# Relational count matrices of a graph network: turned by transposing DMA transfers instead of identity products on TensorE

## The chip, the cores and the metric

The kernel runs on 1 core of one Trainium2 chip. The metric is device time in microseconds of one execution. Three runs of the kernel before took 917.75 us in the median (916.77 to 920.0). A measurement of this kernel can tell a difference of about 0.3% (2.75 us) from none.

## What is computed

Four graph layers act on node features `x` of 1250 nodes by 512, over 21250 directed edges, each of which has one of two types. The third layer is relational: per edge type it has its own 512x512 weight (a mix of 30 basis matrices), a sigmoid gate per source node, and its own sum over neighbours. Cut to what matters here:

```python
edge_index = jnp.stack([src, dst])
x = _layernorm(x + _L0_gnn_ref(x, edge_index, ...))               # degree-normalised sum, batch norm, gelu
x = _layernorm(x + _L1_gnn_ref(x, src, dst, ...))                 # mean over neighbours, two layers
x = _layernorm(x + _L2_gnn_ref(x, edge_index, edge_type_2, ...))  # two rgcn_gate_layer
x = _layernorm(x + _L3_gnn_ref(x, edge_index, ...))               # sum over neighbours

def rgcn_gate_layer(x, row, col, edge_type, basis, att, gate_w, root, bias):
    w = jnp.einsum('rb,bio->rio', att, basis)
    x_j = x[col]
    msgs = [sigmoid(x_j @ gate_w[r, :, 0])[:, None] * x_j @ w[r] for r in range(2)]
    msg = jnp.where((edge_type == 0)[:, None], msgs[0], msgs[1])
    return segment_sum(msg, row, num_segments=N) + x @ root + bias
```

## The kernel before

All sums over neighbours are products with dense count matrices that the kernel builds first. Nodes are padded to 1280, ten tiles of 128. A **window** is 32 destination nodes, so there are 40 windows, four to a tile (`PER`).

**Counting.** For each window VectorE writes one-hot rows of the edges' keys (L1140, L1145, L1151) and TensorE multiplies them (L572, 8 products of 128x320 and 2 more for each further chunk; nearly all windows have 10 or 12 in all) into one of two sets of PSUM banks. ScalarE copies the sums out (`window_out`, L766) into `B`, a buffer for two tiles (j), laid out by source tile, then relation, then column: "p j s r c". TensorE may start window w when window w-2 is copied out (`s_wev`); VectorE may start window w when TensorE is done with window w-2 (`s_win`).

**What becomes of a tile of B.** VectorE adds both relations into `AT` (L1178, `sum_counts`), used by the non-relational layers. For the relational matrix `A` each 128x128 block has to be turned. TensorE does that: `turn_counts` (L597) multiplies four blocks by the identity into one PSUM bank, and ScalarE copies the bank into `A` (`turned_out`, L772). A tile takes five such **turns**, of 20 blocks in all. In the four windows that follow a tile they are done 1, 2, 1, 1 (`COUNT_STEPS`). The last tile's five turns stand inside the first dense products. `A` is first read by unit 3, far behind.

**Beside it.** Between windows TensorE also mixes the first relational layer's basis matrices (L620, 120 products of 128x512 in f32, two instructions each, here called mixes). SP loads a 256 KB matrix for each into 8 slots. Per window there are 2 or 3 mixes (`SHARES`), in eight groups of 15. A group's sum lies in the one bank `T[:, 1]`, and ScalarE copies it out (`mixed_out`, L779); TensorE may begin the next group, and after the last group the first dense product, only when this copy is done (`s_mxe`). Groups end in windows 5, 11, 17, 23, 28, 33 and 39. ScalarE further splits the input (`split_x`, L807 and L809, every second window from 19) and after window 35 the first weight (L863, L866).

**ScalarE's order** is the program's: per window `window_out`, turns out, `mixed_out`, `split_x`. It also issues transfers, among them the transposing ones that already exist (`turn_to`, L828: `S16` tile to a slot of `hT`, 128x1024 f16, 70 of them). Two are issued after window 38, two after window 39, and two at the start of unit 0. While a transfer is issued, what follows on ScalarE waits. The row label ACTq stands for this issuing.

**Unit 0** follows: ten dense tiles (L666), with a product that spreads the degrees (L708), then the aggregation (L721), out-degrees on ScalarE (L1010), batch norm, gelu. Units 1 to 6 follow.

Of the kernel before, what the change touches and what calls it, by code (L numbers as in the profile page):

```python
# [31 lines left out]
COUNT_STEPS = ((0,), (1, 2), (3,), (4,))  # L32
# [16 lines left out]
def resnorm_gnn_kernel(nc, x, src_t, dst_t, typ_t, dst_r, W0, b0, gamma, beta,  # L49
# [11 lines left out]
    with ctx:  # L61
# [101 lines left out]
        B = zview(2 * 2 * NT * REL * P).rearrange("p (j s r c) -> p j s r c", j=2, s=NT, r=REL)  # L163
# [50 lines left out]
        s_at = sem("s_at")  # L214
        s_ate = sem("s_ate")
# [9 lines left out]
        s_eye, s_mixT = sem("s_eye"), sem("s_mixT")  # L225
# [40 lines left out]
        b_idf, b_one, b_dg, b_row, b_rev = (sem("b_" + n) for n in ("idf", "one", "dg", "row", "rev"))  # L266
# [17 lines left out]
        def count_bank(t, g):  # L284

            return (T[:, 0, :], Dp[:, 0, 2, :])[(5 * t + g) % 2]

        LAST_BANKS = [Dp[:, 0, 1, :], Dp[:, 1, 1, :], Dp[:, 0, 2, :]]
# [143 lines left out]
        Z_SCALED = 38  # L432
# [134 lines left out]
        def _(pe):  # L567
# [24 lines left out]
            def turn_counts(t, g, bank):  # L592

                pe.wait_ge(s_wev, PER * (t + 1))
                for r in range(REL):
                    for i in range(2):
                        last = nc.tensor.matmul(bank[:, (2 * r + i) * P:(2 * r + i + 1) * P], B[:, t % 2, 2 * g + i, r, :],  # L597
                                                ident[:, :], start=True, stop=True)
                last.then_inc(s_at, 1)

# [38 lines left out]
            pe.wait_ge(s_mxe, GROUPS)  # L639

            for u, unit in enumerate(UNITS):
                nm, nz = len(unit["mats"]), unit["nz"]

                def dense(t, j):
# [28 lines left out]
                    if u == 0 and t == 0:  # L673
                        degrees(NT - 1)
                        for g in range(3):
                            turn_counts(NT - 1, g, LAST_BANKS[g])
                    if u == 0 and t == 2:
                        for g in range(3, 5):
                            pe.wait_ge(s_ate, 5 * (NT - 1) + g - 2)
                            turn_counts(NT - 1, g, LAST_BANKS[g - 3])  # L680
                    if u == 0 and t == 5:
                        pe.wait_ge(s_ate, 5 * NT)
# [880 lines left out]
```

## Time and profile before

| | us |
|---|---|
| median of 3 runs (lowest, highest) | 917.75 (916.77, 920.0) |
| the profiled execution | 917.2 |
| its span, first to last instruction | 915.4 |
| TensorE busy | 882.8 (96%) |
| VectorE busy | 656.2 (72%) |
| ScalarE busy | 280.8 (31%) |

The span is 1.8 us shorter than the execution's own time. The mean granted clock of TensorE is 0.985 of full speed. The counting stage lasts from 21 us to 184 us, unit 0's dense tiles from 184.6 to 214.

In the rows below, PE is TensorE's products, DVE VectorE, ACT ScalarE, ACTq and SPq the issuing of transfers on ScalarE and SyncE. A row of a timeline begins with start and duration in us; "x10" counts instructions that are merged in it, and the bracket at its end holds the idle time before it and what ended it. Ends of products are modelled: the next product starts before the row's end, so starts are compared with starts.

### The profile page before, as it was taken

How to read it: one execution, taken by the hardware profiler on the slowest of the kernel's cores; microseconds unless marked ns; L12 is line 12 of the kernel's file. 1: busy time of each engine (PE TensorE's matmuls, PEld its weight loads, DVE VectorE, ACT ScalarE, POOL GpSimd, SP SyncE). 2: the span in 40 equal slices, each digit the busy share in tenths (PEclk: the TensorE clock that was granted, in tenths of full speed). 3: DMA queues.
4: the chain of work that ended last, by engine and by line, in shares of the span. 5: the costliest groups of instructions: out<-in, count | busy, mean ns of one | idle time of the engine just before them, and what ended most of it. 6: DMA issues, size and time to landing. Idle time of an engine off the chain costs nothing.

```text
span 915.4 us, 12673 instructions
## 1 busy us (share of the span) xinstructions
PE 882.8 (96%) x4258; PEld 428.2 (47%) x4258; DVE 656.2 (72%) x1286; ACT 280.8 (31%) x431; POOL 87.9 (10%) x66
## 2 busy tenths in 40 slices
PE   7999999999959999899997999999999999999997
PEld 3555555554545444344443444444444444444443
DVE  6898978658987797998999988975324255552247
ACT  0333444637752116222312111114311221132221
POOL 1000111301220003021210000003200020020000
PEclk9999999999979999999998999999999999999999
DMA  8955665596435885788464655530131014322228
GB/s 275 352 168 165 183 188 191 149 238 198 155 95 157 200 236 150 208 207 204 128 150 108 155 141 161 139 91 1 35 81 23 12 47 139 82 62 41 47 60 237
DMA packets 134888, 129.50 MB, mean 141 GB/s; under 512 B 80687, under 2 KB 81156, under 8 KB 134826
## 3 DMA queue, kind: packets, MB, share of 16 engines
q10 hardware_dynamic: 96192, 60.25, 26.1%
q1 hardware_dynamic: 38634, 68.45, 24.9%
q8 instruction: 36, 0.59, 0.3%
q14 instruction: 26, 0.21, 0.1%
HBM read 97.80 MB, written 12.52 MB: 121 GB/s over the span
## 4 chain that ended last, share of the span: by engine, by line
PE 68%; DVE 15%; DMA 8%; ACT 4%; issue 2%; POOL 1%; DVEq 1%; ACTq 0%; SPq 0%
PE Dp L696 25%; PE Dp L666 24%; PE T L620 11%; PE Dp L572 6%; DVE acc L1262 4%; DMA stage<-in_basis 3%; DMA wst<-mixd 2%; DMA xr<-xres 2%; DVE Zraw L1373 1%; ACT W L1010 1%; DVE stt L1354 1%; ACT wst L863 1%; DVE w L1391 1%; PE T L666 1%; POOL Zraw L530 1%
## 5 line engine op out<-in xcount | busy, mean ns | idle before, releaser
L666 PE MATMUL Dp<-W,hT 128*128 128x512 f16 x792 | 175.7, 381 | 3.6 <-DMA hT<-S 3.6
L696 PE MATMUL Dp<-Zraw,A 128*128 128x512 f16 x800 | 173.0, 379 | 0.0
L1262 DVE SCALAR_TENSOR_TENSOR acc<-stage,att,acc 128x512 f32<-128x512 f32 x232 | 163.5, 770 | 4.3 <-DMA stage<-in_basis 4.3
L696 PE MATMUL Dp<-Zraw,AT 128*128 128x512 f16 x600 | 130.0, 379 | 0.0
L666 PEld LDWEIGHTS Dp<-W,hT 128*128 128x128 f16 x792 | 77.8, 98 | 96.6 <-DMA hT<-S 3.8
L696 PEld LDWEIGHTS Dp<-Zraw,A 128*128 128x128 f16 x800 | 78.2, 98 | 94.4
L696 PEld LDWEIGHTS Dp<-Zraw,AT 128*128 128x128 f16 x600 | 58.7, 98 | 70.8
L1140 DVE TENSOR_SCALAR Zraw<-hT,w 128x640 f16<-128x640 f16 (+1 forms) x209 | 85.9, 456 | 0.3
L1391 DVE SCALAR_TENSOR_TENSOR w<-Dp,aggc,S 128x512 f32<-128x512 f32 x40 | 29.9, 747 | 59.9 <-PE Dp L696 54.0
L962 ACT ACTIVATE Zraw<-Dp,zsc 128x512 f16<-128x512 f32 x46 | 29.4, 684 | 125.8 <-PE Dp L666 121.7
L620 PE MATMUL T<-stage,W 128*128 128x512 f32 x120 | 60.5, 627 | 5.5 <-DMA stage<-in_basis 5.5
L572 PE MATMUL Dp<-Zraw 128*128 128x320 f16 (+1 forms) x418 | 63.7, 299 | 0.4 <-DVE Zraw L1140 0.3
L1331 DVE SCALAR_TENSOR_TENSOR Zraw<-Dp,zsc,Zraw 128x512 f16<-128x512 f32 x26 | 19.5, 749 | 58.6 <-ACT Zraw L962 58.6
L1001 ACT ACTIVATE w<-w,s_in 128x512 f32<-128x512 f32 x30 | 21.6, 720 | 121.0 <-DVE w L1391 116.0
L530 POOL TENSOR_TENSOR W<-wst,W 128x1024 f16<-128x1024 f32 x18 | 42.8, 2395 | 158.6 <-ACT W L866 158.6
L572 PEld LDWEIGHTS Dp<-Zraw 128*128 128x128 f16 (+1 forms) x418 | 40.6, 98 | 36.9 <-issue 23.2
L620 PE MATMUL T<-Zraw,W 128*128 128x512 f32 x120 | 57.4, 601 | 0.0
L666 PE MATMUL Dp<-W,stage 128*128 128x512 f16 x240 | 52.8, 379 | 1.2 <-DVE Zraw L1331 1.2
L766 ACT ACTIVATE Zraw<-Dp 128x640 f16<-128x640 f32 x40 | 28.1, 703 | 78.4 <-PE Dp L572 76.3
L721 PE MATMUL Dp<-AT,Zraw 128*128 128x512 f16 (+1 forms) x240 | 43.4, 344 | 0.0
L1151 DVE TENSOR_TENSOR Zraw<-hT,Zraw 128x512 f16<-128x512 f16 x40 | 28.5, 712 | 20.8 <-PE Dp L572 15.0
L962 ACT ACTIVATE Zraw<-Dp 128x512 f16<-128x512 f32 x26 | 15.5, 596 | 74.6 <-PE Dp L666 72.0
(176 smaller groups left out, 950.4 us busy)
## 6 DMA issues: line engine op xcount, KB each, us to landing
stage<-in_basis SPq DMA_DIRECT2D x180, 256.0 KB, 2.9
Zraw<-in_basis SPq DMA_DIRECT2D x60, 256.0 KB, 3.1
xres<-w ACTq DMA_DIRECT2D x30, 256.0 KB, 2.3
xr<-xres ACTq DMA_DIRECT2D x30, 256.0 KB, 3.1
wst<-in_Wn ACTq DMA_DIRECT2D x4, 1024.0 KB, 5.6
wst<-in_Ws ACTq DMA_DIRECT2D x4, 1024.0 KB, 6.0
wst<-mixd ACTq DMA_DIRECT2D x4, 1024.0 KB, 6.0
wst<-in_root ACTq DMA_DIRECT2D x3, 1024.0 KB, 6.7
```

The source lines that it names most:

```text
L530: pool.tensor_tensor(weights_of(u, m)[:, 1, 2 * h:2 * h + 2, :], source, weights_of(u, m)[:, 0, 2 * h:2 * h + 2, :], ALU.subtract).then_in ...
L572: last = nc.tensor.matmul(Dp[:, j, b, 0:HALF], oh_lo[:, ds(slot * P, P)], oh_key[:, ds(slot * KEYS + b * HALF, HALF)], start=start, stop=stop)
L620: nc.tensor.matmul(T[:, 1, :], mixT[:, b * P:(b + 1) * P], mix_in[n % MIX_SLOTS], start=(b == 0), stop=(b == PAIRS - 1)).then_inc(s_mx, 1)
L666: last = nc.tensor.matmul(dense_bank(u, t, m), turned[:, hp, k * P:(k + 1) * P], weights_of(u, m)[:, wp, k, :], start=(n == 0), stop=(n == ...
L696: last = nc.tensor.matmul(sum_bank(t), a[:, k, ds(t * P, P)], Z[:, r, h, k, :], start=(n == 0), stop=(n == count - 1))
L721: last = nc.tensor.matmul(Df[:, j, c:c + w], Z[:, 0, h, k, b * P:(b + 1) * P], AT[:, k, c:c + w], start=(k == 0 and h == 0), stop=(k == NT ...
L766: nc.scalar.activation(B[:, t % 2, :, :, a:a + WIN].rearrange("p s r (b d) -> p b (s r) d", b=2), Dp[:, w % 2, 0:2, 0:HALF].rearrange("p b ...
L962: nc.scalar.activation(Z[:, r, 0, ds(t, 1), :], dense_rows(u, t, r), ACT.Copy, scale=scale).then_inc(s_zhi[u], 1)
L1140: return v.tensor_scalar(oh_key[:, ds(slot * KEYS, KEYS)], iota_n, wkey[:, w:w + 1], key_f[:, ds(c, 1)], ALU.add, ALU.is_equal)
L1151: v.tensor_tensor(oh_lo[:, slot * P:(slot + n) * P].rearrange("p (c k) -> p c k", c=n), iota_n[:, 0:P].rearrange("p (c k) -> p c k", c=1). ...
L1262: last = v.scalar_tensor_tensor(part, stage[:, q, :], a, part, ALU.mult, ALU.add)
L1391: v.scalar_tensor_tensor(w1[:, j:j + 1, :], sum_bank(t).rearrange("p (a d) -> p a d", a=1), c, rest, ALU.mult, ALU.add).then_inc(s_pre[u], 1)
```

## The change

`turn_counts`, `turned_out`, `count_bank`, `COUNT_STEPS` and the semaphores `s_at` and `s_ate` go. In their place ScalarE issues, once the four windows of a tile are copied out, two transposing transfers (`move_counts`), one for each relation, from `B` to `A`: 128x1280 f16 each, 20 in all. `B` is laid out by relation first ("p j r s c"), so that a relation's counts lie in a row; keys are numbered accordingly. Waits on `s_moved` take the place of those on `s_ate`: before ScalarE overwrites a half of `B`, before VectorE's aggregation work of unit 0 (whose data overlay `B`), and before TensorE's first relational aggregation in unit 3. `s_eye` and `b_idf` are folded into the common chain of VectorE.

```diff
-COUNT_STEPS = ((0,), (1, 2), (3,), (4,))
+MOVED = (0, 1)
-        B = zview(2 * 2 * NT * REL * P).rearrange("p (j s r c) -> p j s r c", j=2, s=NT, r=REL)
+        B = zview(2 * 2 * NT * REL * P).rearrange("p (j r s c) -> p j r s c", j=2, s=NT, r=REL)
@@ tensor
-                    for g in COUNT_STEPS[w % PER]:
-                        wait(pe, s_ate, 5 * t + g - 1)
-                        turn_counts(t, g, count_bank(t, g))
                     if w % PER == 2:
                         degrees(t)
                 mix(mix_share(w))
             assert mixed[0] == PAIRS * GROUPS
-            pe.wait_ge(s_ate, 5 * (NT - 1))
             pe.wait_ge(s_mxe, GROUPS)
...
+                    if u == 3 and t == 0:
+                        for i in range(2):
+                            pe.wait_ge(s_moved[i], 16 * len(MOVED) * NT // 2)
@@ scalar, window_out
                 if t > 1 and w % PER == 0:
-                    act.wait_ge(s_ate, 5 * (t - 1))
+                    act.wait_ge(s_moved[t % 2], 16 * len(MOVED) * (t // 2))
@@ scalar
-            def turned_out(t, g, bank):
-                act.wait_ge(s_at, t * 5 + (g + 1))
-                nc.scalar.activation(A[:, :, t, 2 * g * P:2 * (g + 1) * P], bank.rearrange("p (r c) -> p r c", r=REL),
-                                     ACT.Copy).then_inc(s_ate, 1)
+            def move_counts(t):
+
+                act.wait_ge(s_wev, PER * (t + 1))
+                for r in MOVED:
+                    act.dma_start_transpose(A[:, r, t, :].rearrange("p (s n) -> p s n", s=NT),
+                                            B[:, t % 2, r, :, :].rearrange("p s c -> p (s c)")).then_inc(s_moved[t % 2], 16)
@@ scalar, tile_out
                     window_out(w)
-                    if t:
-                        for g in COUNT_STEPS[i]:
-                            turned_out(t - 1, g, count_bank(t - 1, g))
                     if w == NWIN - 1:
                         turn_to(4, 0)
+                    if i == PER - 1:
+                        move_counts(t)
                     for g in range(groups_done(w - 1) if w else 1, groups_done(w)):
                         mixed_out(g)
@@ vector, keys
-            link(v.tensor_copy(key_f, typ_i))
+            link(v.tensor_scalar(key_f, typ_i, float(NT), None, ALU.mult))
...
-            link(v.scalar_tensor_tensor(key_f, src_f, float(REL) / P, key_f, ALU.mult, ALU.add))
+            link(v.scalar_tensor_tensor(key_f, src_f, 1.0 / P, key_f, ALU.mult, ALU.add))
```

ScalarE at the end of the counting stage, windows 36 to 39 and the start of unit 0, in the kernel before:

```order
109 L766 ACTIVATE Zraw<-Dp 128x2x20x16
110 L772 ACTIVATE A<-T 128x2x256
111 L766 ACTIVATE Zraw<-Dp 128x2x20x16
112 L772 ACTIVATE A<-Dp 128x2x256
113 L772 ACTIVATE A<-T 128x2x256
...
118 L828 DMA_TRANSPOSE w<-S 128x8x128 x2
119 L766 ACTIVATE Zraw<-Dp 128x2x20x16
120 L772 ACTIVATE A<-T 128x2x256
121 L828 DMA_TRANSPOSE xr<-S 128x8x128 x2
122 L779 ACTIVATE gw<-T 128x512
123 L782 DMA mixd<-gw 64x512 x2
```

And in the changed kernel, whose L742 is `window_out`, L750 `move_counts`, L757 `mixed_out`, L784 and L786 `split_x`, L805 `turn_to` (`Zraw` holds `B`):

```order
56 L742 ACTIVATE Zraw<-Dp 128x2x20x16 x2
57 L750 DMA_TRANSPOSE A<-Zraw 128x10x128 x2
58 L784 ACTIVATE w<-xr,s_in 128x512
59 L786 ACTIVATE S<-w 128x512
60 L840 ACTIVATE wst<-wst,sW 128x1024 x2
61 L843 ACTIVATE W<-wst 128x1024 x2
62 L742 ACTIVATE Zraw<-Dp 128x2x20x16 x2
...
67 L742 ACTIVATE Zraw<-Dp 128x2x20x16
68 L805 DMA_TRANSPOSE xr<-S 128x8x128 x2
69 L750 DMA_TRANSPOSE A<-Zraw 128x10x128 x2
70 L757 ACTIVATE gw<-T 128x512
```

The copies of turned banks are gone, and behind windows 35 and 39 two longer transposing transfers stand ahead of the splits and ahead of the copy of the last mixed group. Earlier, the same pair stands behind every fourth window; behind windows 11 and 23 it is ahead of `mixed_out` too.

## Rows read from the trace of the kernel before

**Rows 1.** The page: the chain that ended last, by engine.
```profile
PE 68%; DVE 15%; DMA 8%; ACT 4%; issue 2%; POOL 1%; DVEq 1%; ACTq 0%; SPq 0%
```

**Rows 2.** Busy time by stretch: length, PE, PEld, DVE, ACT, POOL, PEclk, DMA share, GB/s.
```profile
60.00:80.00 20.00, 19.63 (x119) 10.91 (x118) 18.62 (x41) 7.05 (x12) 1.24 (x2) 1.00 0.57 166
120.00:160.00 40.00, 40.00 (x220) 22.58 (x219) 31.63 (x78) 17.81 (x31) 5.84 (x4) 1.00 0.58 185
```

**Rows 3.** Timeline of PE: products of windows 1, 2, 7, 8 and 37.
```profile
24.11 1.52 PE L572 MATMUL Dp<-Zraw 128*128 128x320 f16 x10
...
28.04 1.52 PE L572 MATMUL Dp<-Zraw 128*128 128x320 f16 x10
...
46.75 1.52 PE L572 MATMUL Dp<-Zraw 128*128 128x320 f16 x10
...
50.96 1.52 PE L572 MATMUL Dp<-Zraw 128*128 128x320 f16 x10
...
171.21 1.52 PE L572 MATMUL Dp<-Zraw 128*128 128x320 f16 x10
```

**Rows 4.** Timeline of DVE, first keys of windows 8, 9, 14; PE's window 14.
```profile
44.85 0.69 DVE L1151 TENSOR_TENSOR Zraw<-hT,Zraw 128x512 f16<-128x512 f16 x1 [0.74 <-PE Dp L572]
48.49 0.69 DVE L1151 TENSOR_TENSOR Zraw<-hT,Zraw 128x512 f16<-128x512 f16 x1 [1.00 <-PE Dp L572]
...
73.54 0.69 DVE L1151 TENSOR_TENSOR Zraw<-hT,Zraw 128x512 f16<-128x512 f16 x1 [0.62 <-issue]
...
75.09 1.95 PE L572 MATMUL Dp<-Zraw 128*128 128x320 f16 x10 [0.27 <-DVE Zraw L1140]
```

**Rows 5.** Timeline, windows 23 and 24: PE's products, ACT's copy of a mixed group.
```profile
111.08 1.52 PE L572 MATMUL Dp<-Zraw 128*128 128x320 f16 x10
...
115.49 0.60 ACT L779 ACTIVATE gw<-T 128x512 f32<-128x512 f32 x1 [1.66 <-PE T L620]
```

**Rows 6.** Timeline of PE, window 35, and of ACT behind it until window 36 is out.
```profile
163.37 1.52 PE L572 MATMUL Dp<-Zraw 128*128 128x320 f16 x10
...
166.01 0.72 ACT L807 ACTIVATE w<-xr,s_in 128x512 f32<-128x512 f32 x1
...
167.30 2.17 ACT L863 ACTIVATE wst<-wst,sW 128x1024 f32<-128x1024 f32 x2
...
171.27 0.68 ACT L766 ACTIVATE Zraw<-Dp 128x640 f16<-128x640 f32 x1
```

**Rows 7.** Timeline: PE in windows 38 and 39, ACT, and PE's first dense product.
```profile
175.65 1.52 PE L572 MATMUL Dp<-Zraw 128*128 128x320 f16 x10
...
179.28 1.52 PE L572 MATMUL Dp<-Zraw 128*128 128x320 f16 x10
...
184.57 2.75 PE L666 MATMUL Dp<-W,w 128*128 128x512 f16 x12 [0.91 <-issue]
...
182.47 1.30 ACTq L828 DMA_TRANSPOSE xr<-S  x1
183.87 0.60 ACT L779 ACTIVATE gw<-T 128x512 f32<-128x512 f32 x1 [1.84 <-PE T L620]
```

**Rows 8.** Timeline of ACT: issuing of transposing transfers, 128x1024 f16 each.
```profile
185.73 1.51 ACTq L828 DMA_TRANSPOSE hT<-S  x1
...
187.28 3.34 ACTq L828 DMA_TRANSPOSE hT<-S  x1
...
363.38 1.25 ACTq L828 DMA_TRANSPOSE Zraw<-S  x1
```

**Rows 9.** Busy time by stretch, columns as in rows 2: one microsecond of such transfers.
```profile
179.00:180.00 1.00, 1.00 (x8) 0.53 (x6) 0.00 (x0) 0.00 (x0) 1.00 (x2) 1.00 1.09 207
```

**Rows 10.** Chain that ended last, in order of time: a window's products, the last tile's turns.
```profile
167.75 1.63 PE Dp L572 x12
...
187.55 0.69 PE Dp L597 x12
...
193.42 0.45 PE Dp L597 x8
```

More of the change, by code:

```diff
@@ L213, in resnorm_gnn_kernel @@
         s_wev = sem("s_wev")
-        s_at = sem("s_at")
-        s_ate = sem("s_ate")
+        s_moved = [sem(f"s_moved{j}") for j in range(2)]
         s_xin, s_xmax, s_s0 = sem("s_xin"), sem("s_xmax"), sem("s_s0")
@@ L224, in resnorm_gnn_kernel @@
         e_att = sem("e_att")
-        s_eye, s_mixT = sem("s_eye"), sem("s_mixT")
+        s_mixT = sem("s_mixT")
         mx_full = [sem(f"mx_full{i}") for i in range(MIX_SLOTS)]
@@ L265, in resnorm_gnn_kernel @@
         s_xst = {u: [sem(f"s_xst{u}_{j}") for j in range(2)] for u in LN}
-        b_idf, b_one, b_dg, b_row, b_rev = (sem("b_" + n) for n in ("idf", "one", "dg", "row", "rev"))
+        b_one, b_dg, b_row, b_rev = (sem("b_" + n) for n in ("one", "dg", "row", "rev"))
         b_ev, b_st, b_mv, b_sd, b_co, b_g = (sem("b_" + n) for n in ("ev", "st", "mv", "sd", "co", "g"))
@@ L431, in resnorm_gnn_kernel @@
         XS_FROM = 19
-        Z_SCALED = 38
+        Z_SCALED = 39
         def halves_split(u):
@@ L590, in window @@
                 pair_product(FIXED * (w % 2) + 1, j, stop=True).then_inc(s_win, 1)
[L592 to L599, printed above, removed]
             def degrees(t):
@@ L674, in dense @@
                         degrees(NT - 1)
[L675 to L680, printed above, removed]
                     if u == 0 and t == 5:
-                        pe.wait_ge(s_ate, 5 * NT)
                         spread()
@@ L763, in window_out @@
                 if t > 1 and w % PER == 0:
-                    act.wait_ge(s_ate, 5 * (t - 1))
+                    act.wait_ge(s_moved[t % 2], 16 * len(MOVED) * (t // 2))
                     act.wait_ge(s_sum, 2 * (t - 1))
-                nc.scalar.activation(B[:, t % 2, :, :, a:a + WIN].rearrange("p s r (b d) -> p b (s r) d", b=2),
+                nc.scalar.activation(B[:, t % 2, :, :, a:a + WIN].rearrange("p r s (b d) -> p b (r s) d", b=2),
                                      Dp[:, w % 2, 0:2, 0:HALF].rearrange("p b (d k) -> p b k d", k=REL * NT),
                                      ACT.Copy).then_inc(s_wev, 1)
-            def turned_out(t, g, bank):
-                act.wait_ge(s_at, t * 5 + (g + 1))
-                nc.scalar.activation(A[:, :, t, 2 * g * P:2 * (g + 1) * P], bank.rearrange("p (r c) -> p r c", r=REL),
-                                     ACT.Copy).then_inc(s_ate, 1)
+            def move_counts(t):
[3 more added lines that the diff above has]
+                                            B[:, t % 2, r, :, :].rearrange("p s c -> p (s c)")).then_inc(s_moved[t % 2], 16)
             def mixed_out(g):
@@ L980, in first_z @@
                     z_out(t, j)
-                    if u == 0 and t in (0, 2):
-                        for g in range(3) if t == 0 else range(3, 5):
-                            turned_out(NT - 1, g, LAST_BANKS[g % 3])
                     if u == 0 and t == 6:
@@ L1087, in _ @@
             dve.wait_ge(s_const, 8)
-            v.tensor_tensor(eye, ident[:, 0:P // 2], ident[:, P // 2:P], ALU.add).then_inc(s_eye, 1)
-            dve.wait_ge(s_eye, 1)
+            link(v.tensor_tensor(eye, ident[:, 0:P // 2], ident[:, P // 2:P], ALU.add))
             def mix_table(a0, a1):
@@ L1177, in sum_counts @@
                 dve.wait_ge(s_wev, PER * (t + 1))
-                v.tensor_tensor(AT[:, :, t * P:(t + 1) * P], B[:, t % 2, :, 0, :], B[:, t % 2, :, 1, :], ALU.add).then_inc(s_sum, 1)
+                v.tensor_tensor(AT[:, :, t * P:(t + 1) * P], B[:, t % 2, 0, :, :], B[:, t % 2, 1, :, :], ALU.add).then_inc(s_sum, 1)
                 dve.wait_ge(s_sum, 2 * t + 1)
@@ L1314, in _ @@
                 dve.wait_ge(s_mxst[j], 16 * REL * GROUPS // 2)
-            v.tensor_copy(identf, ident[:, :]).then_inc(b_idf, 1)
-            dve.wait_ge(b_idf, 1)
+            link(v.tensor_copy(identf, ident[:, :]))
             for t in range(NT):
@@ L1482, in _ @@
                     dve.wait_ge(s_bn, 48)
+                    for i in range(2):
+                        dve.wait_ge(s_moved[i], 16 * len(MOVED) * NT // 2)
                     weight_work("agg", 0, 0)
```

4 lines of the change are left out of this document (removed).

## The prediction

> **What bounds the kernel now.** I read the chain of waits first: two thirds of it lie on TensorE [rows 1]. The change touches TensorE only in the counting stage (21 to 184 us) and in unit 0's first dense tiles, so the busy times by stretch come next. TensorE is busy all the time from 120 to 160, while VectorE has 31.6 of 40 us and ScalarE 17.8; from 60 to 80 VectorE is at 18.6 of 20 too [rows 2]. So the reader is to see a stage bound by TensorE, with a stretch in it where VectorE has almost no room. The timelines of both engines then say what a turn costs and where VectorE waits, and ScalarE's timeline says what it holds when others wait for it.
>
> **What a turn costs TensorE.** Windows 1, 7 and 37 each have 10 window products and 3 mixes until the next window starts, and 0, 1 and 2 turns. From start to start they take 28.04 - 24.11 = 3.93, 50.96 - 46.75 = 4.21 and 175.65 - 171.21 = 4.44 us [rows 3, 7]. A turn is 0.28 us where it stands alone, two are 0.51. Twelve window products run 1.63 us [rows 10], so ten run 1.36 and a mix (3.93 - 1.36) / 3 = 0.86. A tile's five in windows with 1, 2, 1, 1 are 3 x 0.28 + 0.51 = 1.35; I take 1.3, as the third of these windows has the degree product too, and keeps a part of the change-over between kinds of product. Nine tiles hold 11.7 us of turns in the counting stage. The copies that go from ScalarE (45 there, 5 later) are not on the path.
>
> **How much of that VectorE lets through.** VectorE waited for TensorE 0.74 and 1.00 us before windows 8 and 9, then works without such a wait until window 14's keys, which TensorE waits for itself, by 0.27 us [rows 4]. A faster TensorE brings VectorE to window 14 earlier by at most those 1.74 us, and TensorE has saved about 1.3 by window 8: I take **1.0 us** at window 14 (bounds 0 and 1.74). From there to window 39 are 25 windows, 6.25 tiles: 6.25 x 1.3 = **8.1 us**. In windows 15 to 20 VectorE is still near its limit; of the two, one catches the other again, and I take **1.0 us** off (bounds 0 and 2.5, the saving of two tiles). TensorE would reach the end of window 39 earlier by 1.0 + 8.1 - 1.0 = 8.1 us, if nobody else held it.
>
> **What the moves cost ScalarE.** The kernel has 70 transposing transfers of 128x1024. Their issue holds ScalarE 1.25 us where the queue is empty, 1.30 in a row of four, and 1.51 and 3.34 when the basis loads of the next stage press on it [rows 7, 8]. No row shows one of 128x1280. If issue goes by size it is 1.56, if it doesn't it is 1.25; beside the basis loads of the counting stage, which take 0.57 of the transfer engines [rows 2], I take **1.7 us**. The lower end is 1.25, the upper 3.34. As for the transfers themselves, 1.09 of the 16 engines' time gave 207 GB/s [rows 9], so 327,680 bytes take some 1.6 us and two per tile 3.3 in each 15 us: the share goes from 0.57 to about 0.8. The mixes' loads have eight slots, some 12 us of work ahead. I cost that at nothing; if that cover goes, TensorE waits for basis matrices.
>
> A pair is issued when its window's copy is done, some 1.0 us after the window's last product, so it holds ScalarE until 1.0 + 3.4 = 4.4 us behind that. Queued behind it are the copy of a mixed group, the splits and the next window's copy. Four places matter.
> - **Window 11.** The group's copy comes late, but what TensorE loses is lost before window 14, where it waits for VectorE anyway: nothing.
> - **Window 23.** It ends at 111.08 + 1.36 = 112.44 and the copy of the group came at 115.49, just behind the mixes [rows 5]. Now it is done at 4.4 + 0.6 + 0.1 = 5.1 us behind the window. TensorE wants the bank after 3 mixes of 0.86 and window 24's twelve products (1.63): 4.2. Cost **0.9 us**.
> - **Window 35.** It ends at 164.73. A split (1.4) and the first weight's scaling (167.30 to 171.27, 4.0) came ahead of window 36's copy [rows 6]. With the pair it begins at 4.4 + 1.4 + 4.1 = 9.9 and is seen at 10.8 us. Window 38 needs it, and TensorE, without turns, is there at 2.57 + 1.63 + 1.71 + 1.36 + 2.57 = 9.8. Cost **1.0 us**.
> - **Window 39.** It ends at 180.64. Four transposing transfers were issued until 183.77, then the last group was copied and the first dense product began at 184.57, 3.93 us behind the window [rows 7]. The pair now goes between: the first at 1.7 as elsewhere, the second under the basis loads of the next stage, which start with the last mix. The 3.34 us of rows 8 is the second in that state; with less queued I take 3.1. So 3.13 + 0.1 + 4.8 + 0.8 for the copy and its hand-overs is 8.8 us, and the cost is 8.8 - 3.9 = **4.9 us** (bounds 2.6 with two issues of 1.25, and 6.8 with two of 3.34).
>
> **The dense tiles.** TensorE goes through the last tile's turns in 0.69 + 0.45 = **1.1 us** [rows 10], which are rows of the chain that ended last, so this is gained. Dense tile 4 needs tile 0 of the first aggregation's input from ScalarE and VectorE; ScalarE has the fifth and sixth turned tile to issue ahead of that, as before. Unit 0's later steps start from the end of the dense tiles and shift with them. The waits on `s_moved` ask for data that landed long ago. The new order of `B` changes no instruction's size.
>
> **The sum.** -8.1 + 0.9 + 1.0 + 4.9 - 1.1 = -2.4 us. Against the profiled execution that is 917.2 - 2.4 = 914.8; this execution lies 0.55 below the median, so on the scale of the medians it is **915.3 us**. All that hangs on one number: with every issue at x us the three stalls are 2(x - 1.25), 2(x - 1.2) and 2x + 0.1, and the sum is 6x - 14.0.
>
> **Two rules of the Trainium skill.** Rows 3 give 0.28 us for four blocks on TensorE, and rows 9 some 1.6 us of all transfer engines for ten. "VectorE: DVE Perf Modes" (Rules for kernel authors) advises TensorE for turning 128x128 where PSUM will do as the place of the result, and the transfer otherwise. It speaks against this change, and rows 3 and 9 agree with its direction; by it the moves are the dearer path, which is the second rival. "Advanced Engine Details and Errata" (X-Bar Transpose (TRN2)) says transposing transfers run as fast as plain ones, at 350 to 400 GB/s. The 207 GB/s of rows 9 don't agree; by its figure a move would take an estimated 0.8 to 0.9 us and hardly queue, which is the first rival.
>
> **Rivals.**
> - *No back-pressure, the last pair costs what others do.* At 1.56 us each, 6 x 1.56 - 14.0 = -4.6; at 1.25, -6.5. That is 911.2 to 913.1. For it: four in a row went at 1.25 to 1.34 without one being held. Against: 3.34 in rows 8, in that very place.
> - *Transfers hold ScalarE everywhere; slower.* From x = 2.33 on the sum is positive. The ring may be short, and each pair is issued beside 256 KB loads. At 3.0 it is +4.0, and group copies at window 28 come late too, about +5.5: 921.8 to 923.3. TensorE's idle time would stand ahead of mixes, put down to ScalarE's copy. Against: the rows with light traffic show 1.25.
> - *VectorE becomes the bound.* If it binds until window 24, where before it waited little, 2.5 us instead of 1.0 are lost: -0.9, 916.9; with a call on the loads, 918.
>
> **How the numbers follow.** Forecast (913.2 to 917.5) 0.45, no back-pressure 0.25, back-pressure everywhere 0.17, VectorE or loads 0.13. About 0.3% (2.75 us) is what a measurement can tell. Faster by more than that, below 915.0: all of the second case and four tenths of the first, 0.25 + 0.17 = 0.42. Slower, above 920.5: most of the third case and a little of the last, 0.20. The same: 0.38. The range reaches from the first rival's best, 910.8, to 922.0, which takes in most of the second and leaves out its worst.
>
> **What would show it.** In the changed profile: windows 7 and 37 some 0.28 and 0.5 us shorter; window 14 earlier by about 1 us and the end of window 39 by about 6, at 174.4; issues of `move_counts` near 1.7 us, the last near 3; TensorE idle ahead of the first dense product for some 5 us, put down to ScalarE or to issue; the transfer share between 120 and 160 near 0.8. I am wrong if an issue takes over 2.3 us in the middle of the stage, if TensorE waits for basis matrices, or if the end of window 39 moves by less than 4 us.

## The result, and the profile after

| | us |
|---|---|
| after: median of 4 runs (lowest, highest) | 933.42 (929.44, 935.47) |
| before: median of 4 runs (lowest, highest) | 917.87 (916.77, 920.0) |
| ratio (95% interval) | 1.0168 (1.0142 to 1.0193) |
| the profiled execution after, its span | 935.15, 933.3 |

The changed kernel is slower by some 15.5 us. The forecast was 915.3 with a range up to 922.0, so the prediction was wrong, in sign too. The changed kernel also spreads more: its four runs lie 6.0 us apart, those of the kernel before 3.2.

**Where the time went.** The chain that ended last, by engine (it answers to [rows 1]):

```profile
PE 61%; DVE 16%; DMA 6%; ACTq 6%; ACT 6%; issue 2%; POOL 1%; SPq 0%; DVEq 0%
```

ScalarE's issuing (ACTq) went from 0% to 6% of the span, TensorE from 68% to 61%. What TensorE waited for between 5 and 300 us (engine and line, what it waited for, total us, times, longest us):

```profile
PE Dp L647 <- ACT gw L757: 10.5, 1, 10.5
PE T L605 <- DMA stage<-in_basis: 6.4, 2, 5.4
PE Dp L566 <- ACT Zraw L742: 5.0, 3, 3.1
PE T L605 <- ACT gw L757: 4.4, 2, 2.4
```

Of the 6.4 us on basis matrices 5.4 lie at the start and stand in the kernel before too (5.5). The rest is new: 10.5 us ahead of the first dense product (L647), 5.0 us ahead of window products (L566) and 4.4 us ahead of mixes (L605), all on a copy of ScalarE, and 1.1 us on a basis matrix. ScalarE's timeline says why those copies are late:

```profile
33.60 11.36 ACTq L750 DMA_TRANSPOSE A<-Zraw  x2
45.01 1.30 ACT L742 ACTIVATE Zraw<-Dp 128x640 f16<-128x640 f32 x2 [11.44 <-issue]
...
52.83 9.16 ACTq L750 DMA_TRANSPOSE A<-Zraw  x2
...
104.02 3.41 ACTq L750 DMA_TRANSPOSE A<-Zraw  x2
...
118.38 4.40 ACTq L750 DMA_TRANSPOSE A<-Zraw  x2
123.21 0.60 ACT L757 ACTIVATE gw<-T 128x512 f32<-128x512 f32 x1 [4.86 <-issue]
...
187.60 2.85 ACTq L805 DMA_TRANSPOSE xr<-S  x2
190.49 7.73 ACTq L750 DMA_TRANSPOSE A<-Zraw  x2
198.33 0.60 ACT L757 ACTIVATE gw<-T 128x512 f32<-128x512 f32 x1 [10.10 <-issue]
```

The ten pairs of moves held ScalarE 11.36, 9.16, 6.40, 3.39, 3.41, 4.40, 3.45, 3.41, 3.76 and 7.73 us. In the middle of the stage a move costs mostly 1.7 us, as forecast (2.2 in the sixth pair); in the first three pairs and the last it costs about two to three times that. The shortest single issue took 1.35 us. At the end of the stage, on TensorE (it answers to [rows 7]):

```profile
184.38 1.52 PE L566 MATMUL Dp<-Zraw 128*128 128x320 f16 x10
...
198.98 4.42 PE L647 MATMUL Dp<-W,w 128*128 128x512 f16 x12 [10.51 <-ACT gw L757]
...
203.49 2.75 PE L647 MATMUL Dp<-W,w 128*128 128x512 f16 x12
```

Window 39's products end at 184.38 + 1.36 = 185.74 (before 180.64, forecast 174.4), and the first dense product starts 13.24 us behind that (before 3.93, forecast 8.8). The first twelve dense products then take 4.42 us and the next 2.75: after the long idle time TensorE started at the lower level of its clock (the mean from 190 to 200 is 0.61, see below; from 199 to 202 it is 0.50). The clock fell at two more places, inside the counting stage. The rows are a window behind a wait of 3.09 us, two mix instructions behind a wait of 2.05 us (elsewhere 1.52 and 1.02 us), and the stretch from 124 to 125 with a granted clock of 0.50:

```profile
45.77 2.85 PE L566 MATMUL Dp<-Zraw 128*128 128x320 f16 x10 [3.09 <-ACT Zraw L742]
...
123.86 2.07 PE L605 MATMUL T<-stage,W 128*128 128x512 f32 x2 [2.05 <-ACT gw L757]
```

```profile
124.00:125.00 1.00, 1.00 (x2) 0.48 (x3) 0.54 (x1) 0.00 (x0) 0.00 (x0) 0.50 1.27 288
```

Up to the next window's start they cost some 1.4 us (4.77 instead of the 3.41 that the same products take from 165.10) and 1.8 us (4.36 instead of 2.58 for three mixes).

Busy time by stretch, columns as in [rows 2], of the kernel before:

```profile
20.00:30.00 10.00, 10.00 (x45) 5.41 (x44) 6.56 (x24) 2.41 (x4) 0.00 (x0) 1.00 1.03 375
30.00:40.00 10.00, 10.00 (x49) 5.47 (x49) 7.95 (x21) 2.20 (x4) 0.00 (x0) 1.00 1.06 385
40.00:50.00 10.00, 10.00 (x62) 5.78 (x60) 8.27 (x24) 4.67 (x8) 0.00 (x0) 1.00 0.69 215
60.00:70.00 10.00, 10.00 (x60) 5.73 (x59) 9.96 (x22) 4.05 (x7) 0.35 (x1) 1.00 0.56 162
```

and after:

```profile
40.00:50.00 10.00, 6.91 (x30) 3.37 (x30) 5.47 (x16) 2.49 (x4) 0.00 (x0) 0.83 1.15 199
...
60.00:70.00 10.00, 7.84 (x41) 3.52 (x40) 9.51 (x22) 2.22 (x4) 0.00 (x0) 1.00 1.20 126
...
120.00:160.00 40.00, 37.95 (x171) 20.21 (x170) 30.98 (x75) 12.70 (x20) 5.23 (x4) 0.96 0.85 224
...
190.00:200.00 10.00, 1.02 (x3) 0.43 (x4) 0.00 (x0) 0.60 (x1) 0.00 (x0) 0.61 1.11 201
```

From 40 to 80 us the transfer engines are busy throughout (1.13 to 1.20, where 0.56 to 0.69 stood before), and between 60 and 70 they move fewer bytes, 126 GB/s instead of 162. Between 120 and 160 the share is 0.85; I had said about 0.8.

### The profile page after: what moved, and what is told of

It reads as the page before. It is cut to its first block, busy times and chain, and to the rows that moved or that the text cites. A ratio compares the mean times of both kernels' runs of the same rounds, so it can differ in the third digit from the quotient of the medians.

```text
span 933.3 us, 12200 instructions
## 1 busy us (share of the span) xinstructions
PE 877.0 (94%) x4058; PEld 416.9 (45%) x4058; DVE 656.3 (70%) x1286; ACT 256.2 (27%) x381; POOL 86.7 (9%) x66
## 4 chain that ended last, share of the span: by engine, by line
PE 61%; DVE 16%; DMA 6%; ACTq 6%; ACT 6%; issue 2%; POOL 1%; SPq 0%; DVEq 0%
PE Dp L673 24%; PE Dp L647 22%; PE T L605 8%; PE Dp L566 5%; DVE acc L1235 5%; ACTq L750 5%; DMA stage<-in_basis 2%; DVE stt L1326 1%; DVE Zraw L1345 1%; ACT wst L840 1%; ACTq L805 1%; ACT W L984 1%; DMA wst<-mixd 1%; DVE w L1363 1%; DMA xr<-xres 1%
## 5 line engine op out<-in xcount | busy, mean ns | idle before, releaser
L647 PE MATMUL Dp<-W,hT 128*128 128x512 f16 x792 | 176.9, 383 | 3.8 <-DMA hT<-S 3.5
L647 PEld LDWEIGHTS Dp<-W,hT 128*128 128x128 f16 x792 | 77.8, 98 | 97.8 <-issue 3.8
L566 PE MATMUL Dp<-Zraw 128*128 128x320 f16 (+1 forms) x418 | 65.7, 303 | 6.1 <-ACT Zraw L742 5.0
L605 PE MATMUL T<-stage,W 128*128 128x512 f32 x120 | 61.4, 633 | 8.5 <-DMA stage<-in_basis 6.4
L566 PEld LDWEIGHTS Dp<-Zraw 128*128 128x128 f16 (+1 forms) x418 | 40.7, 99 | 44.6 <-issue 23.3
L605 PE MATMUL T<-Zraw,W 128*128 128x512 f32 x120 | 57.6, 603 | 2.4 <-ACT gw L757 2.4
L647 PE MATMUL Dp<-W,stage 128*128 128x512 f16 x240 | 52.8, 379 | 1.2 <-DVE Zraw L1303 1.2
L742 ACT ACTIVATE Zraw<-Dp 128x640 f16<-128x640 f32 x40 | 27.7, 700 | 86.1 <-PE Dp L566 57.6
L647 PE MATMUL Dp<-W,wst 128*128 128x512 f16 x144 | 34.2, 402 | 4.9 <-DVE S L1311 4.9
```

The costliest lines, as they stand in the source:

```text
L566: last = nc.tensor.matmul(Dp[:, j, b, 0:HALF], oh_lo[:, ds(slot * P, P)], oh_key[:, ds(slot * KEYS + b * HALF, HALF)], start=start, stop=stop)
L605: nc.tensor.matmul(T[:, 1, :], mixT[:, b * P:(b + 1) * P], mix_in[n % MIX_SLOTS], start=(b == 0), stop=(b == PAIRS - 1)).then_inc(s_mx, 1)
L647: last = nc.tensor.matmul(dense_bank(u, t, m), turned[:, hp, k * P:(k + 1) * P], weights_of(u, m)[:, wp, k, :], start=(n == 0), stop=(n == ...
```

## The experiments

Theory 1: what ScalarE's queue holds while a move is issued is the cost, above all where other loads press on the transfer engines, and behind window 39. 1a says that it is the turning that makes a move dear there, 1b that any transfer of that size would be. The rivals are the new layout, VectorE as the bound, and missing basis matrices. Times of before in the same sessions were 917.29 to 918.17 in the median. "Gap" is the time from the end of window 39's products to the first dense product. Where a kernel has added lines, its line numbers differ.

| kernel | time (median) | ratio (interval) | w14 out | w39 ends | gap |
|---|---|---|---|---|---|
| before | 917.87 | 1 | 77.08 | 180.64 | 3.93 |
| after | 933.42 | 1.0168 (1.0142 to 1.0193) | 84.98 | 185.74 | 13.24 |
| plain copies | 911.79 | 0.9931 (0.9914 to 0.9947) | 76.93 | 173.93 | 5.35 |
| no moves | 912.09 | 0.9935 (0.9911 to 0.9959) | 76.16 | 175.03 | 4.50 |
| few loads (one run) | 920.22 | | 76.81 | 175.29 | 11.23 |
| first two tiles turned | 920.6 | 1.003 (1.0018 to 1.0041) | 77.63 | 176.95 | 10.69 |
| last pair late | 923.2 | 1.0057 (1.0036 to 1.0079) | 82.19 | 182.91 | 5.31 |
| groups first | 921.98 | 1.0046 (1.0027 to 1.0065) | 81.87 | 182.20 | 4.23 |
| spread | 917.97 | 0.9996 (0.9979 to 1.0013) | 78.31 | 178.82 | 4.41 |
| hybrid | 915.51 | 0.9965 (0.9949 to 0.9982) | 76.83 | 177.44 | 5.17 |
| hybrid, GpSimd later | 913.38 | 0.9954 (0.9935 to 0.9972) | 77.73 | 178.92 | 5.85 |
| the same, copy first | 913.22 | 0.9955 (0.9939 to 0.997) | 76.39 | 174.33 | 3.48 |

(Window 14's copy starts and window 39's products end at the times given, in us of the profiled execution. That execution can lie off the median: for "GpSimd later" it took 921.38 us, the slowest of seven, so the three places in its row are not typical of it.)

**Only the layout.** The kernel before, with the diff's new order of `B` and of the keys:

```diff
-        B = zview(2 * 2 * NT * REL * P).rearrange("p (j s r c) -> p j s r c", j=2, s=NT, r=REL)
+        B = zview(2 * 2 * NT * REL * P).rearrange("p (j r s c) -> p j r s c", j=2, s=NT, r=REL)
```

> The kernel before with the second part of the change alone: B and the keys lie by relation first, and TensorE turns the blocks as before. Theory: the order of B costs nothing, since no copy, sum or product changes its size: copies of a window 0.70 us, sums 0.82 us, 917 to 919 us, the same. Rival: the window's copy or the sum into AT is dearer or cheaper by its new strides; 0.2 us on each of 40 copies or 10 sums would move the time by 1 us or more.

It took 918.21 us, ratio 0.9998 (0.9979 to 1.0018). The order of `B` costs nothing.

**Moves left out, first try.** `move_counts` and the waits on it go, and GpSimd fills `A` with zeros:

```diff
             pool.memset(ones, 1.0).then_inc(b_one, 1)
+            pool.memset(A[:, :, :, :].rearrange('p r t n -> p (r t n)'), 0.0).then_inc(b_one, 1)
...
-                    if i == PER - 1:
-                        move_counts(t)
```

> The changed kernel without its 20 moves: A is set to zero by GpSimd once instead (part left out: the relational counts). Theory 1 (the moves' issue holds ScalarE, and TensorE waits for the copies queued behind it): without them TensorE keeps what the turns cost: end of window 39 some 8 us before the kernel before's 180.6 (172 to 173), first dense product 3.9 us behind it, whole kernel 9.2 us faster than before: about 908.6. Rival (VectorE is the limit once the turns are gone): window 39 ends at 176 or later and the kernel is at 912 or above.

It took 931.92 us, ratio 1.0147 (1.0129 to 1.0165), for a cause that I had put in myself. GpSimd's timeline, and the waits of TensorE:

```profile
11.46 21.52 POOL L513 MEMSET A<- 128x25600 f16 x1
```

```profile
PE Dp L567 <- DVE Zraw L1108: 22.5, 4, 18.0
```

While GpSimd filled `A` for 21.5 us, one small operation of VectorE ahead of its first keys (L1090, 128x40) took 21.52 us instead of 0.18. The keys came late by that, and TensorE waited up to 18.0 us for them. As a test of the moves it says nothing; its gap, 199.56 - 195.08 = 4.5 us, is that of the next kernel.

**Moves left out, second try.** No filling; the relational sums read `AT` instead:

```diff
-                    rels = [(A[:, r], r) for r in range(REL)] if nz == 2 else [(AT, 0)]
+                    rels = [(AT, r) for r in range(REL)] if nz == 2 else [(AT, 0)]
...
-                    if i == PER - 1:
-                        move_counts(t)
```

> The changed kernel without any move; the relational sums read AT in place of A, which has the same shape (part left out: the relational counts). Step of the prediction under test: what the turns cost TensorE and how much of it VectorE lets through. By the prediction window 39 is out 8.1 us before the kernel before and the kernel takes 908.6. With what e2_plain_copies showed (window 39 out 6.7 us earlier, no gain at window 14), 908 to 910. Rival (the plain copies of e2 cost nothing, VectorE alone took the difference): within 1 us of e2_plain_copies, 911 to 912.

912.09 us, with no wait on ScalarE inside the counting stage. The prediction's 908.6 and the theory's 908 to 910 were missed; the rival's number came, within 1 us of the plain copies below. This is the change without its price. Window 14 came 77.08 - 76.16 = 0.92 us earlier, window 38 7.4 us earlier (169.78 instead of 177.20), and window 39 5.6 us. The last two microseconds went to a collision. VectorE's keys of window 39, and GpSimd beside them:

```profile
169.28 2.11 DVE L1112 TENSOR_SCALAR Zraw<-hT,w 128x128 f16 x1
171.31 3.00 DVE L1107 TENSOR_SCALAR Zraw<-hT,w 128x640 f16 x3
```

```profile
169.13 4.29 POOL L524 TENSOR_TENSOR W<-wst,W 128x1024 f16<-128x1024 f32 x2
```

The keys at L1112 take 0.24 and the three at L1107 1.15 us elsewhere. In the kernel before, GpSimd's subtractions (the low parts of the first weight) ran from 176.91, when VectorE's last keys had been written. They start straight behind GpSimd's own part of the last input split. Without two copies of turned banks between window 37's copy and that split they start 3.3 us behind window 37's copy instead of 4.1, and VectorE's keys of window 39 start 1.9 us behind it instead of 0.8, so the two meet. "SBUF — State Buffer" of the Trainium skill (SBUF: two separate sides) says that for VectorE operations of some kinds (those in a two-port mode, and some with two inputs in SBUF) and any GpSimd operation, whichever starts first holds the ports that they share for its whole instruction. 2.11 us beside GpSimd instructions of some 2.1 us each agrees with it; that the keys are of such a kind is not shown otherwise.

**Plain copies of the same bytes.** This leaves the number, the size and the place of the transfers, and takes the turning away:

```diff
-                    act.dma_start_transpose(A[:, r, t, :].rearrange("p (s n) -> p s n", s=NT),
-                                            B[:, t % 2, r, :, :].rearrange("p s c -> p (s c)")).then_inc(s_moved[t % 2], 16)
+                    act.dma_start(A[:, r, t, :],
+                                  B[:, t % 2, r, :, :].rearrange("p s c -> p (s c)")).then_inc(s_moved[t % 2], 16)
```

> The changed kernel with each move as a plain SBUF-to-SBUF copy of the same 327,680 bytes, at the same places on the same queue (part left out: the turning). Theory 1a (it is the transposing kind of transfer that is slow and holds its issuer when the basis loads press): issues of 0.3 to 1 us each, no waits of TensorE for ScalarE's copies, 908 to 911 us. Rival 1b (any transfer of this size that meets SP's loads is held): the first three pairs and the last one hold ScalarE 5 to 11 us as in the changed kernel, 925 to 933 us.

911.79 us, just outside the theory's 908 to 911: all but nothing is lost against the kernel without moves. One wait of TensorE for ScalarE is left, 2.61 us ahead of the first dense product. Its timelines of ScalarE and TensorE:

```profile
33.01 1.17 ACTq L750 DMA_DIRECT2D A<-Zraw  x2
```

```profile
179.28 2.76 PE L647 MATMUL Dp<-W,w 128*128 128x512 f16 x12 [2.61 <-ACT gw L757]
```

Where the turning pair held ScalarE for 11.36 us, two plain copies take 1.17, in the same traffic. The third part of the profiles' pages gives the engine time: the queue of these transfers has 26.1% of 915.4 us before, 28.5% of 911.0 with plain copies and 31.0% of 933.3 after. Twenty plain copies add 20.7 us, 1.0 each; twenty moves add 50.4, 2.5 each, where I had estimated 1.6 (part of this may be other transfers of that queue that take longer beside them). That is 1a; 1b falls. The two kinds differ in one more thing: a move adds 1312 packets to its queue, some 250 bytes each, and a plain copy 144, some 2.3 KB each. A plain copy in packets of that size was not run, so whether it is the turning or the small packets that are dear stays open.

**Few loads.** The moves as in the changed kernel, but only the first eight basis matrices are loaded:

```diff
-                for n in range(first, end):
+                for n in range(first, min(end, MIX_SLOTS)):
```

> The changed kernel with only the first 8 of the 120 basis matrices of the first relational layer loaded; the other mixes read the same slots again (part left out: their data). The moves then meet an idle queue, but for the x tiles at the start and the next stage's loads at the last pair. Theory 1 (basis loads of SP hold the moves): each pair holds ScalarE about 3.1 us or less, the first one too, TensorE waits for ScalarE by 2 us or less before window 39, which is out before 176. Rival 1d (a transposing transfer of this size holds its issuer by itself): first pairs of 6 us and more as in the changed kernel. The time isn't compared with 917, since loads are missing; window 39 and the pairs are.

One run took 920.22 us. The first pair and one in the middle, and one microsecond of such transfers alone:

```profile
32.98 3.13 ACTq L751 DMA_TRANSPOSE A<-Zraw  x2
...
96.88 2.95 ACTq L751 DMA_TRANSPOSE A<-Zraw  x2
```

```profile
99.00:100.00 1.00, 1.00 (x9) 0.77 (x8) 1.00 (x5) 0.12 (x1) 0.00 (x0) 1.00 1.08 200
```

Nine pairs take 2.91 to 3.81 us (11.36 has become 3.13), and only the last, beside the loads of the next stage, 6.96. So it is the moves beside loads that hold ScalarE for long. TensorE waited 1.8 us for ScalarE's copies before window 39, as the theory said. Alone, a pair occupies all engines for 0.96 + 1.08 + 1.15 + 0.31 = 3.5 us between 98 and 102, 1.75 us per move at 188 to 208 GB/s. Here the second issue of a pair takes 2.95 - 1.35 = 1.6 us, about as long as one move occupies the engines. That it waits for the first move to get through is my reading; no row shows the wait itself.

**The last pair late.** Only the last tile's pair goes behind dense tile 8's output:

```diff
-                    if i == PER - 1:
+                    if i == PER - 1 and t < NT - 1:
                         move_counts(t)
...
                     z_out(t, j)
+                    if u == 0 and t == 8:
+                        move_counts(NT - 1)
```

> The changed kernel with only the last tile's pair moved to another place: behind dense tile 8 of unit 0, in place of ahead of the last mixed group's copy. Prices the turnover. Theory 1: the first dense product starts some 4 to 5 us behind window 39's last product (13.2 in the changed kernel), the time falls by 8 to 9 us: 923 to 926. Rival (the transposing transfers of the next tiles are themselves held by the basis loads): it starts 8 us or more behind, 928 or above.

923.2 us, 933.4 - 923.2 = 10.2 us less, and the gap is 5.31. Not all of it is the last pair's place. In the profiled executions the gap is 7.9 us shorter and the dense tiles 1.3 us (the clock stays up), 9.3 together. But window 39 already ends 2.8 us earlier, though up to there the two programs are the same: the first pair takes 12.54 us, the second and third 4.57 and 3.55, where the changed kernel's took 9.16 and 6.40. How long early pairs are held differs from execution to execution by that much.

**The first two tiles turned.** Tiles 0 and 1 are turned on TensorE as before, the other pairs stay where the change puts them:

```diff
-                    if i == PER - 1:
+                    if i == PER - 1 and t >= TURNED:
                         move_counts(t)
```

> The changed kernel with tiles 0 and 1 turned by TensorE as before, all others in pairs at the places of the changed kernel. Prices the first two pairs, which held ScalarE 11.4 and 9.2 us. Theory 1: window 14 is out at 77 to 78 (84.98 in the changed kernel; VectorE's own time), so 6 to 8 us come back: 925 to 928. Rival (the third pair and the later ones take over what the first two cost): 930 or above.

920.6 us: the first two pairs cost 12.8 us, against 6 to 8 expected. Window 14 is back at 77.63, and the third pair shrank with them, from 6.40 to 4.11:

```profile
65.45 4.11 ACTq L780 DMA_TRANSPOSE A<-Zraw  x2
...
180.31 6.53 ACTq L780 DMA_TRANSPOSE A<-Zraw  x2
```

10.2 and 12.8 add up to 23.0, more than the 21.3 us between the changed kernel and the one without moves. By places of the profiled executions, window 39 ends 8.8 us earlier here, and 2.6 more come from a shorter gap, though the last pair stands where it was. So each price carries some 2 to 3 us that are not its own, and I read them as about half and half.

**Groups first.** The copy of a mixed group goes ahead of the pair:

```diff
-                    if i == PER - 1:
-                        move_counts(t)
                     for g in range(groups_done(w - 1) if w else 1, groups_done(w)):
                         mixed_out(g)
+                    if i == PER - 1:
+                        move_counts(t)
```

> The changed kernel with the copy of a finished mixed group ahead of the tile's moves on ScalarE; nothing else is changed. Theory 1: TensorE's waits for that copy go (4.4 us in the counting stage, 10.5 ahead of the first dense product), but the last pair, held some 8 us, now delays the turned tiles 4 and 5 and the first output of the dense tiles, so about 4 us come back as a wait inside the dense tiles: 920 to 924 us. Rival 2 (load on the transfer engines is the cost, wherever ScalarE stands): the time hardly moves, 930 or more.

921.98 us, inside the theory's range. The gap is back at 4.23, but the pair, which holds ScalarE for 4.88 us, now delays the outputs of the first dense tiles, and TensorE waits 2.5 us at dense tile 4. In the counting stage its waits for the group copies go, and 4.1 us of waits for window copies stay. The first pairs take 10.56 and 7.33 us, much as before. The fourth and fifth take 7.42 and 7.60 us, where the changed kernel's took 3.39 and 3.41, in the middle of the stage. The fourth pair is issued at 89.40 there and at 86.28 here. The first whole microsecond behind the issue, in the changed kernel and in this one:

```profile
90.00:91.00 1.00, 1.00 (x3) 0.29 (x2) 1.00 (x4) 0.00 (x0) 0.00 (x0) 1.00 0.35 39
```

```profile
87.00:88.00 1.00, 1.00 (x4) 0.36 (x3) 1.00 (x3) 0.00 (x0) 0.00 (x0) 1.00 0.98 332
```

There it met a gap between two bundles of basis loads, here it met a bundle. So the middle of the stage isn't cheap by itself; what a pair costs goes with the traffic at its moment of issue.

**Spread.** One move at a time, behind windows 4t + 4 and 4t + 6; the last tile's behind the outputs of dense tiles 7 and 8:

```diff
-                    if i == PER - 1:
-                        move_counts(t)
...
+                    if t and i in (0, 2):
+                        move_counts(t - 1, (i // 2,))
...
                     z_out(t, j)
+                    if u == 0 and t in (7, 8):
+                        move_counts(NT - 1, (t - 7,))
```

> The changed kernel with its moves issued one at a time: of each tile the first behind the first window of the next tile, the second behind its third, always behind the copy of a mixed group; the last tile's two behind dense tiles 7 and 8. Theory 1 (a second transfer issued behind a first that hasn't moved holds ScalarE): issues near 1.35 us, hardly any wait of TensorE for ScalarE, 909 to 913 us, so faster than before. Rival 2 (20 transfers of about 2.5 us of all engines' time starve the mixes of basis matrices): TensorE waits for those loads by 5 us or more and the time is 917 or above.

917.97 us, ratio 0.9996: the theory's 909 to 913 was missed. A single issue takes 1.35 to 1.5 us mostly, but not among the first:

```profile
43.80 5.27 ACTq L750 DMA_TRANSPOSE A<-Zraw  x1
```

A move then landed up to 15.6 us after its issue, so that window 8's copy waited for the buffer `B` until 59.52 (52.52 before), and window 39 lost more to the collision with GpSimd. The time is near the rival's, by another mechanism: TensorE waited only 1.6 us for basis matrices.

**Hybrid.** Spread, and tiles 0 and 1 turned on TensorE.

> Tiles 0 and 1 of B are turned by TensorE as in the kernel before (their moves met the saturated transfer engines, 20 to 60 us); tiles 2 to 9 are moved one transfer at a time as in e4_spread. Theory 1 (loss comes from moves issued into a busy queue, and ten turns ahead of window 14, where TensorE waits for VectorE anyway, cost nothing): issues of 1.35 to 1.5 us, window 39 out at 173 to 175 (180.84 in the kernel before, 179.02 in e4_spread), 910 to 913 us. Rival 2 (the load of transposing transfers on the engines costs TensorE's loads wherever they stand): 916 or above.

915.51 us, ratio 0.9965 (0.9949 to 0.9982): the first version that beats the kernel before by a measurable amount, though the interval doesn't exclude less than the 0.3% that I had named. It missed the theory's 910 to 913, and window 39's copy starts at 177.65, not 173 to 175. Issues take 1.34 to 2.46 us, 1.4 in the median. It has the collision with GpSimd:

```profile
170.19 3.44 DVE L1148 TENSOR_SCALAR Zraw<-hT,w 128x640 f16<-128x640 f16 x2
173.56 2.11 DVE L1153 TENSOR_SCALAR Zraw<-hT,w 128x128 f16 x1
```

```profile
171.25 4.37 POOL L532 TENSOR_TENSOR W<-wst,W 128x1024 f16<-128x1024 f32 x2
```

**GpSimd later.** The hybrid, and GpSimd's subtractions wait for the last keys:

```diff
+            pool.wait_ge(s_oh, FIXED * NWIN)
             low_weights(0, 0)
```

> e5_hybrid with one more wait: GpSimd starts the low half of the first weight only when VectorE has written its last keys. In e5 and e6 two 128x1024 subtractions of GpSimd (4.4 us) run while VectorE writes window 39's keys, and a key operation there takes 2.1 to 2.6 us in place of 0.25 to 0.4. Theory 3 (the two engines hold each other up, and window 39 is late by that): keys back at 0.25 to 0.4 us, window 39 out near 175 (177.65 in e5), 912 to 914 us. Rival (GpSimd's result, now later, is what the first dense product waits for): window 39 is out earlier but the first dense product still starts near 182.6, 915 to 916.

913.38 us, ratio 0.9954 (0.9935 to 0.9972). The keys at those two lines take 0.80 and 0.25 us again, so the collision is gone; the interval overlaps the hybrid's, so the 2.1 us between the medians are likely, not shown. Its profiled execution, the slow one of 921.38 us, doesn't show the earlier end of window 39 (its copy starts at 181.02). The next kernel, which is the same up to there, does: 175.45, as forecast.

**Copy first.** In window 39 the last group's copy also goes ahead of the turned input tiles:

```diff
-                    if w == NWIN - 1:
-                        turn_to(4, 0)
                     for g in range(groups_done(w - 1) if w else 1, groups_done(w)):
                         mixed_out(g)
+                    if w == NWIN - 1:
+                        turn_to(4, 0)
```

> e9b_pool_later with the copy of the last mixed group ahead of the two transposing transfers that are issued behind window 39. Theory 1 (what stands ahead of that copy on ScalarE is what the first dense product waits for, transfers of before included): the first dense product starts 3.9 to 4.2 us behind window 39's last product (5.9 in e9b), 911 to 913 us, against 917.4 of the kernel before. Rival (dense tiles 2 to 5 then wait for their turned input, issued later by 0.7 to 1 us): the start moves, the end of the dense tiles doesn't, and the time is that of e9b, 913 to 914.

913.22 us, ratio 0.9955. TensorE's timeline and waits:

```profile
177.81 2.75 PE L670 MATMUL Dp<-W,w 128*128 128x512 f16 x12 [0.73 <-ACT gw L788]
```

```profile
PE T L670 <- DMA xr<-S: 1.4, 1, 1.4
```

The gap is 3.48, the shortest of all, but dense tile 2 waits 1.4 us for its turned input, which stands behind the copy now. The gain of one wait went into another, as the rival said. This version and the one before it are some 4 to 5 us faster than the kernel before and 20 faster than the changed one. The kernel before with only this last order of copies was not run.

## Why the prediction was wrong

**What held.**
- *The turns' price.* Windows of 10 products and 3 mixes take 3.93 us, as said. The kernel without moves gained 6.5 us between windows 14 and 38 (7.4 - 0.92), where 7.1 net was forecast up to window 39.
- *Window 14 is pinned by VectorE.* 1.0 was forecast, 0.92 measured; without moves TensorE waits 2.63 us for VectorE there (0.27 before).
- *Windows 23 and 35.* 0.9 and 1.0 us were forecast. TensorE's waits there were 2.05 us (at 123.86, on the copy of the group) and 0.72 us (at 180.61, on window 36's copy): 2.8 instead of 1.9.
- *The dense tiles.* From the first dense product to the aggregation it took 29.49 before and 28.39 with plain copies, 1.1 less, as forecast.
- *The layout.* Nothing, as said.

**What failed.** The sum forecast -2.4 us; the profiled executions differ by 933.3 - 915.4 = 17.9. The 20.3 between lie here:

| place | forecast | measured | miss |
|---|---|---|---|
| window 14's copy | -1.0 | +7.9 | 8.9 |
| window 14 to the end of window 39 | -5.2 | -2.8 | 2.4 |
| gap | +4.9 | +9.3 | 4.4 |
| dense tiles | -1.1 | +0.6 | 1.7 |
| behind them | 0 | +2.9 | 2.9 |

- *The first three pairs (8.9 us).* The step that failed was "Window 11 ... nothing", and with it that only four places matter. I priced every issue at 1.7 us from rows in light traffic, and costed contention of the transfers at nothing, with a share of 0.57 [rows 2] that is the share of 60 to 80. In the kernel before it is 1.03 and 1.06 from 20 to 30 and from 30 to 40 (above), where the first pair would be issued, at 33.6. The first three pairs held ScalarE for 11.36, 9.16 and 6.40 us instead of 3.4. TensorE waited 3.1, 1.2, 0.7, 1.1 and 2.4 us between 45 and 78, 8.5 in all, and lost 1.4 more at the lower clock; the slack at window 14, where TensorE waits 2.63 us for VectorE without moves, was far too small for that. The kernel with few loads and the one with its first tiles turned both put window 14 back at 77; this term is shown.
- *The last pair (4.4 us).* The place and the sign were right, the size was not. The pair started 4.75 us behind the window instead of 3.13, since the four transposing transfers ahead of it took 3.74 and 2.85 us, and it held the copy for 7.8 us instead of 4.8. My upper bound for the cost, 6.8 from [rows 8], was too low against the 9.3 that came: it took the longest of a few rows for the longest that can be.
- *The dense tiles (1.7 us).* I did not think of the clock: the first twelve products took 4.42 instead of 2.75 us.
- *Behind them (2.9 us).* From the start of the aggregation to the end it took 701.3 us before and 704.3 after, and 700.5 to 705.3 in the other kernels, not in the order of their moves. The kernel with only the new layout, which has no move, took 703.9 there, so nothing ties these 2.9 us to the change.
- *Windows 14 to 39 (2.4 us).* 0.9 are the two waits named above; the lower clock behind the wait at 123.86 took some 1.8 more, which makes up the rest.

Two slips of arithmetic in the prediction bear on nothing: four tenths of 0.45 are 0.18, not 0.17, and the first rival's best is 911.2, not 910.8. The 1.6 us for a move is the time that its bytes take at 207 GB/s; with the share of 1.09 it is 1.7 us of engine time, close to the 1.75 measured alone.

**The rivals.** "Transfers hold ScalarE everywhere; slower" had the sign and the mechanism, and got 0.17. Even its price of +5.5 was a third of what came, and "everywhere" was wrong for the kernel as changed: in the middle of the stage the issue stayed near 1.7 us. Its break-even was stated as one number x, when x differs by place; with x = 5.7, 4.6 and 3.2 for the first three pairs and 3.9 for the last, no average decides. VectorE or the basis loads as the bound cost 1.1 us in one wait. The rule of "VectorE: DVE Perf Modes" (Trainium skill, Rules for kernel authors), to turn 128x128 on TensorE where PSUM will do as the place of the result, pointed the right way for this change, though the fastest versions here move eight tiles of ten by transfers, one at a time. The 350 to 400 GB/s of "Advanced Engine Details and Errata" (Trainium skill, X-Bar Transpose (TRN2)) is not reached by the moves of this case: 188 to 208 GB/s alone, and 327,680 bytes in 2.5 us, or 131 GB/s, in the mean of the changed kernel.

## What to carry to other kernels

A transposing transfer that is issued by a compute engine held that engine for 1.35 us or for 9.0, depending on the traffic. So price each one by the traffic at its own place, with the transfer share in slices of 10 us rather than that of the stage, and list what stands behind it. Plain copies in the same places cost next to nothing. What helped here was to issue the transposing ones singly, behind the work that others wait for, and to keep the turning on TensorE where the transfer engines are already full. A wait of TensorE can cost more than its length, by the clock behind it. When a change takes work off an engine, look also at what starts earlier for it (here GpSimd's subtractions, into VectorE's keys).

## What the runs showed of the hardware

- A transposing transfer of 128x1280 f16 holds ScalarE 1.35 us where there is room, and the second of a pair 1.6 to 2.0 behind it; in full traffic the second took up to 9.0 us. Of plain copies of the same bytes two take 1.17 us in the first pair's place (one issue 0.50 to 1.63 us over the kernel). Per move the engines spend 1.75 us alone and 2.5 us in the mean of the changed kernel, against 1.0 for the plain copy.
- GpSimd held VectorE for whole instructions: beside a fill of 128x25600 f16 on GpSimd (21.5 us) a VectorE operation of 0.18 us took 21.52, and beside subtractions of 2.1 us keys of 0.25 took 2.11.
- After TensorE had idled for 2.6 us or less ahead of the first dense product, its twelve products took 2.75 us. After 8.0, 8.5 and 10.5 us of idling (first two tiles turned, few loads, after) they took 5.18, 4.92 and 4.42, at the lower level of the clock, and after 3.11 us (GpSimd later) 4.17. The idle time just before doesn't settle it alone: in the changed kernel's counting stage the granted clock stood at 0.50 from 124 to 127, behind a wait of only 2.05 us.
